# Another steady order for the first attention: scores and both mixes back to back, two turns fewer, GpSimd normalising the inputs

## The reference

```python
x = x + tanh(g_xattn[0]) * L0_xattn(ctx_1024, layernorm(x), mask, ...)   # the part that is changed
x = x + tanh(g_ffn[0])   * L0_ffn(layernorm(x), ...)                     # 16 experts, top 8 tokens each, and a shared one
x = x + tanh(g_xattn[1]) * L1_xattn(layernorm(x), ctx_1024, ctx_1024, ...)
x = x + tanh(g_ffn[1])   * L1_ffn(layernorm(x), ...)                     # ternary weights, 8 bit activations
```

```python
x = layer_norm(x, ...); latents = layer_norm(latents, ...)
q = latents @ Wq
k, v = split(concatenate([x, latents]) @ Wkv)
q = l2norm(q) * q_scale;  k = l2norm(k) * k_scale
sim = where(full_mask, einsum(q, k) * 8.0, -max)
out = einsum(softmax(sim), v)
return layer_norm(out @ Wo, ln_o_w, ln_o_b)
```

## Time and profile before

| | us |
|---|---|
| median of 3 runs | 406.26 (404.84 to 407.8) |
| span of the profiled execution | 402.5 |
| TensorE busy in it | 372.5 (93%) |
| VectorE busy | 328.7 (82%) |
| ScalarE busy | 257.7 (64%) |
| GpSimd busy | 226.0 (56%) |

### The profile page before, as it was taken

The page is one execution under the profiler, slowest core; times in us unless marked ns, Lnnn a source line. Parts: engine busy times, 40 slices in busy tenths (PEclk is TensorE's granted clock), DMA queues, the critical chain, the costliest instruction groups (busy, mean ns, idle before and its releaser), DMA issues. The chain is left out here.

```text
span 402.5 us, 10554 instructions
## 1 busy us (share of the span) xinstructions
PE 372.5 (93%) x3612; PEld 274.0 (68%) x3612; DVE 328.7 (82%) x925; ACT 257.7 (64%) x514; POOL 226.0 (56%) x372
## 2 busy tenths in 40 slices
PE   8799999999999999999999999999698999996766
PEld 8356666667666667668756888778477777775545
DVE  4889999899989999988483788564659999998995
ACT  2577777778777777776664222345377777777784
POOL 4564668766676666663322000056649999887850
PEclk9999999999999999999999999999999999999598
DMA  5969999700000000000000000000000000000003
GB/s 155 259 148 119 132 133 131 83 2 2 0 3 1 2 2 2 2 0 2 3 2 0 2 0 2 0 2 0 2 2 2 2 5 2 2 2 2 2 15 91
DMA packets 61283, 13.27 MB, mean 33 GB/s; under 512 B 51488, under 2 KB 60592, under 8 KB 61232
## 3 DMA queue, kind: packets, MB, share of 16 engines
q1 hardware_dynamic: 59776, 11.94, 19.6%
q10 hardware_dynamic: 1328, 0.66, 0.6%
q0 software_dynamic: 128, 0.00, 0.0%
HBM read 11.55 MB, written 1.05 MB: 31 GB/s over the span
## 5 line engine op out<-in xcount | busy, mean ns | idle before, releaser
L397 POOL TENSOR_TENSOR a_rn<-a_ssq,neghalf 128x8 f32<-128x8 f32 x48 | 79.0, 1653 | 29.8 <-DVE a_ssq L996 25.2
L996 DVE TENSOR_REDUCE a_ssq<-q_home 128x8 f32<-128x512 f32 x48 | 32.3, 672 | 6.5 <-ACT q_home L783 6.5
L91 POOL TENSOR_TENSOR moments<-moments,eps_row 128x1 f32<-128x1 f32 x32 | 6.2, 193 | 54.9 <-DVE moments L86 54.7
L486 PE MATMUL a_x<-wkv_a,a_kvT 128*128 128x512 f32 x64 | 34.5, 621 | 0.9 <-ACT kv_home L789 0.8
L789 ACT ACTIVATE kv_home<-a_x,maskcol 128x512 f32<-128x512 f32 x32 | 21.9, 684 | 19.1 <-PE a_x L486 19.1
L413 POOL TENSOR_TENSOR a_yr<-a_ymv,eps_row 128x1 f32<-128x1 f32 x16 | 3.0, 191 | 38.0 <-DVE a_ymv L1039 38.0
L1846 DVE TENSOR_REDUCE b_mx<-b_s 128x16 f32<-128x1024 f32 x16 | 19.6, 1223 | 5.3 <-PE b_s L1489 5.3
L1015 DVE TENSOR_REDUCE a_mx<-a_s 128x4 f32<-128x512 f32 x32 | 21.9, 686 | 2.0 <-PE a_s L512 1.9
L1343 POOL TENSOR_TENSOR b_k<-b_ksb,quad 128x256 f32<-128x256 f32 x32 | 18.9, 613 | 7.9 <-ACT b_ksb L1682 7.9
L531 PE MATMUL a_m<-kv_home,p_home 128*64 128x65 f32 x512 | 22.4, 228 | 0.7 <-issue 0.4
L801 ACT ACTIVATE kv_home<-a_m,cols 128x512 f32<-128x512 f32 x32 | 21.9, 685 | 0.8 <-PE a_m L500 0.7
(11 more groups left out here) (292 smaller groups left out, 1163.2 us busy)
## 6 DMA issues: line engine op xcount, KB each, us to landing
w_gu<-in_L_ffn_Wg_dram SPq DMA_DIRECT2D x4, 512.0 KB, 9.0
w_gu<-in_L_ffn_Wu_dram SPq DMA_DIRECT2D x4, 512.0 KB, 10.7
w_d<-in_L_ffn_Wd_dram SPq DMA_DIRECT2D x8, 256.0 KB, 7.8
out_dram<-xs SPq DMA_DIRECT2D x8, 128.0 KB, 1.8
xs<-in_x_dram SPq DMA_DIRECT2D x1, 640.0 KB, 11.3
cs<-in_ctx_dram SPq DMA_DIRECT2D x1, 640.0 KB, 11.1
wkv_a<-in_L_xattn_Wkv_dram SPq DMA_DIRECT2D x1, 512.0 KB, 7.7
nat<-in_L_ffn_w_dram SPq DMA_DIRECT2D x2, 256.0 KB, 3.1
```

The costliest lines, as they stand in the source:

```text
L397: nc.gpsimd.tensor_tensor(rn[:, tp, i, :], ssq[:, tp, i, :], neghalf[:, 0:H0], ALU.pow)\
L486: nc.tensor.matmul(p_x[:], kvT[:, tp, b * 2 * S:(b + 1) * 2 * S], wkv_a[:, INNER:2 * INNER], start=True, stop=True).then_inc(vproj_done, 1)
L996: nc.vector.tensor_reduce(ssq[:, tp, i, :], sq[:, i, :].rearrange("p (h d) -> p h d", h=H0), AX.X, ALU.add).then_inc(reduced, 1)
```

## The change

The loops of all four engines get another order, and `TURNS` ends two turns earlier (22 to 20). TensorE does both `probs_T` of tile s-2 and both `mix` of it in turn s, the mixes right behind the `scores` of tile s-1; `xT` of tile s+1 stands ahead of these scores. VectorE begins its turn with both `row_max`, both `attend`, both `shift`; the reductions and scales of tile s now lie in turn s itself, with `scale(s, 0)` right behind `reduce(s, 0)`. `normalise` moves from VectorE to GpSimd from the third tile on. For this the mean is kept with a minus sign and added. GpSimd does the powers of a tile in two turns, with `inverse_root` and `out_norm` between the first and the second. The diff, shortened:

```diff
-        TURNS = range(2, NT + 7)
+        TURNS = range(2, NT + 5)
...
+            def normalise(t, tp):
+                wait(pool, xT_done, t - 1 if t > 2 else t)
+                nc.gpsimd.tensor_scalar(xn[:, tp, 0, :], cs[:, t, :], moments[:, 0, t, 0:1], moments[:, 0, t, 1:2],
+                                        ALU.add, ALU.mult)
+                nc.gpsimd.tensor_scalar(xn[:, tp, 1, :], xs[:, t, :], moments[:, 1, t, 0:1], moments[:, 1, t, 1:2],
+                                        ALU.add, ALU.mult).then_inc(xn_ready, 1)
+
             inverse_roots(0)
             for i in range(3):
                 inverse_norm(0, 0, i)
             inverse_roots(1)
+            pool.wait_ge(norms_ready, 2)
+            normalise(2, 0)
+            inverse_norm(1, 1, 0)
+            inverse_norm(1, 1, 1)
             for s in TURNS:
+                if exists(s - 1, NT):
+                    inverse_norm(s - 1, (s - 1) % 2, 2)
+                if s == 5:
+                    inverse_roots(2)
+                    pool.wait_ge(norms_ready, 3)
+                if exists(s + 1, NT):
+                    normalise(s + 1, (s + 1) % 2)
+                if exists(s - 2, NT):
+                    weigh(s - 2, s % 2)
                 if exists(s - 4, NT):
                     add_bias(s - 4, s % 2)
...
+                if exists(s, NT):
+                    inverse_norm(s, s % 2, 0)
+                if exists(s - 5, NT):
+                    inverse_root(pool, s - 5).then_inc(root_ready, 1)
                 if exists(s - 4, NT):
                     out_norm(s - 4, s % 2)
+                if exists(s, NT):
+                    inverse_norm(s, s % 2, 1)
...
+                if exists(s - 2, NT):
+                    probs_T(s - 2, 1)
+                if exists(s + 1, NT):
+                    xT(s + 1, (s + 1) % 2)
                 if exists(s - 1, NT):
                     scores(s - 1, (s - 1) % 2)
+                if exists(s - 2, NT):
+                    mix(s - 2, s % 2, 0)
+                    mix(s - 2, s % 2, 1)
...
                 if exists(s - 2, NT):
                     exp(s - 2, 0)
+                    exp(s - 2, 1)
...
                 if exists(s - 2, NT):
                     row_max(s - 2, 0)
+                    row_max(s - 2, 1)
                 if exists(s - 3, NT):
                     attend(s - 3, 0)
                     attend(s - 3, 1)
+                if exists(s - 2, NT):
+                    shift(s - 2, 0)
+                    shift(s - 2, 1)
+                if exists(s - 1, NT):
+                    scale(s - 1, (s - 1) % 2, 2)
                 if exists(s, NT):
                     replace_masked(s, s % 2)
...
+                if exists(s, NT):
+                    reduce(s, s % 2, 0)
+                    scale(s, s % 2, 0)
+                    reduce(s, s % 2, 1)
+                if exists(s - 4, NT):
+                    write_output(s - 4, s % 2)
+                if exists(s - 5, NT):
+                    next_input(s - 5)
+                if exists(s, NT):
+                    reduce(s, s % 2, 2)
+                    scale(s, s % 2, 1)
```

More of the change, by code:

```diff
@@ L1117, in _ @@
             later = sum(GROUPS[2]) // 2
-            for s in TURNS:
-                if exists(s - 1, NT):
-                    reduce(s - 1, (s - 1) % 2, 0)
-                if exists(s, NT):
-                    for i, (first, _) in enumerate(GROUPS):
-                        if s == first:
-                            dve.wait_ge(norms_ready, i + 1)
-                    normalise(s, s % 2)
-                if exists(s - 1, NT):
-                    reduce(s - 1, (s - 1) % 2, 1)
-                if exists(s - 5, NT):
-                    write_output(s - 5, (s - 5) % 2)
-                if exists(s - 1, NT):
-                    scale(s - 1, (s - 1) % 2, 0)
+            reduce(1, 1, 0)
+            reduce(1, 1, 1)
+            scale(1, 1, 0)
+            reduce(1, 1, 2)
+            scale(1, 1, 1)
+            for s in TURNS:
                 if exists(s - 2, NT):
                     row_max(s - 2, 0)
-                if exists(s - 1, NT):
-                    reduce(s - 1, (s - 1) % 2, 2)
-                    scale(s - 1, (s - 1) % 2, 1)
-                if exists(s - 2, NT):
-                    shift(s - 2, 0)
+                    row_max(s - 2, 1)
                 if exists(s - 3, NT):
```

51 lines of the change are left out of this document (12 added, 39 removed).

## The result

| | before | after |
|---|---|---|
| median of 4 runs each, side by side, us | 405.55 (403.83 to 407.8) | 431.38 (429.09 to 433.23) |
| span of the profiled execution | 402.5 | 429.5 (that run: 432.3) |
| TensorE busy | 372.5 (93%) | 373.7 (87%) |
| VectorE busy | 328.7 (82%) | 322.9 (75%) |
| ScalarE busy | 257.7 (64%) | 255.5 (59%) |

After to before is 1.063 (95% interval 1.058 to 1.068): slower, near the 430 us of the prediction.

The account below looks back on a forecast made before the run. The prediction took TensorE to bound the kernel before, and a VectorE-GpSimd loop of 11.64 us after. Span 402.5 + 21.2 (through turn 15) + 2.4 (tail) = 426.1, plus 3.8 to the median: 430 us, range 419 to 438.

Parts of the forecast that it names:

- The loop: VectorE and GpSimd waits, key scale to key scale: 11.64 us a turn, 12.04 or 12.30 with weight transposes.
- A to R: VectorE, from key scale scale(s,1) to the next turn's query reduction reduce(s+1,0): 5.96 us without weight transposes.
- R to A: From query reduction over GpSimd's two powers and two pairs back to the key scale: 5.68 us.
- The sum along A: Key-scale starts added turn by turn through the first attention; turn 15's at 196.0 us, 21.2 later than before.
- A(2) to A(5): Key-scale starts of turns 2 to 5 on VectorE, forecast at 35.2, 45.8, 59.0 and 73.9 us.
- A(1): Start of turn 1's key scale on VectorE, after GpSimd's normalise and two powers: 25.9 us.
- the price of GpSimd's normalise: Two 128x128 operations on GpSimd: 1.20 us together, hidden in steady turns.
- the one-off work: Small work in turns 5 and 6 and turn 2's squares: 0 to 1.5 us together, taken as 0.7.
- Its own turn: TensorE's turn in the new order: from 10.79 us to 10.64, or 10.45 at best.
- The tail: Turn 15's key scale to last logits: near 27.3 us, 2.4 later than before, between -3 and +4.
- A(15): Start of turn 15's key scale on VectorE: 196.0 us, where before it was 174.78.
- The clock rival: TensorE idles more, its granted clock falls in the tail, matmuls double: 438 to 442 us; chance 8%.

Follow-up runs that it names:

- e1: Kernel after, with reduce(s,1) ahead of scale(s,0) on VectorE; 426.81 us, 1.051 of before.
- e2: Kernel after, with normalise put back on VectorE between reduce(s,0) and scale(s,0); 431.23 us, 1.064 of before.
- e3: Kernel after, with the powers of inverse_norm replaced by a multiplication (output differs); 405.2 us, 0.998 of before.
- y1: Kernel before, with turn_queries on TensorE moved behind both mixes instead of between them; 405.9 us, ratio 1.001.
- e4: Kernel before, with the powers of inverse_norm replaced by a multiplication (output differs); 405.28 us, ratio 0.997.
- e5: Kernel after, with GpSimd's inverse_root and out_norm behind the second power and VectorE's reductions, scales reordered; 433.37 us, 1.071 of before.
- x1: Kernel after, with both GpSimd powers first, VectorE reordered, write_output a turn later, one turn more; 428.19 us, 1.053 of before.
- x3: Kernel after reordered as in x1, plus read_output ahead of reduce(s,0), write_output and row_stats on VectorE; 415.52 us, 1.023 of before.
- y4: Kernel before with TensorE's whole new order, and on VectorE a reduction before row_max, read_output before a shift and next_input; 407.87 us, 1.004.

## Why the prediction was right, and where not

**The loop.** A to R was to be 5.96 us without weight transposes. Measured 129.59 - 123.21 = 6.38, of which 0.42 is a transpose (123.82 to 124.24): 5.96. R to A was to be 5.68 and is 5.59. So the turns are 11.97 and 12.23 where 12.04 and 12.30 were written down. That this loop sets them is shown by its pieces, which add up to the turn without a gap, and by e1 and e2 (moving or adding work in its gap changes a turn by 0.04 at most). That the powers make it so long is shown by e3. It worked because each piece had a row of its own in the trace of before; only their order was new.

**The sum along A**, from the timeline of VectorE: the key scales of turns 1, 7, 8 and, by the last row, 15:

```profile
25.21 0.69 DVE L1023 SCALAR_TENSOR_TENSOR q_home<-a_rn,a_y 128x512 f32<-128x512 f32 x1 [0.32 <-POOL a_rn L397]
...
98.23 0.69 DVE L1023 SCALAR_TENSOR_TENSOR q_home<-a_rn,a_y 128x512 f32<-128x512 f32 x1 [0.34 <-POOL a_rn L397]
110.98 0.69 DVE L1023 SCALAR_TENSOR_TENSOR q_home<-a_rn,a_y 128x512 f32<-128x512 f32 x1 [0.34 <-POOL a_rn L397]
...
195.80 0.69 DVE L1023 SCALAR_TENSOR_TENSOR q_home<-a_rn,a_y 128x512 f32<-128x512 f32 x1 [0.34 <-POOL a_rn L397]
```

The forecast had 25.9, 97.1, 110.0 and 196.0; in between, A(2) to A(5) were 35.04, 46.13, 59.28 and 74.19 against 35.2, 45.8, 59.0 and 73.9. That they lie so close is in part luck. A(1) came 0.7 earlier than forecast; turns 2 and 3 then took 9.83 and 11.09 where 9.25 and 10.55 were laid out. Of the 0.7 at A(1), 0.3 is that GpSimd was free earlier (normalise starts at 21.09, not 21.39). The step that failed is the price of GpSimd's normalise, taken as 0.60 for each of two from the earlier trace rows, which makes 0.3 more. It measured 0.44 from start to start:

```profile
124.79 0.45 POOL L419 TENSOR_SCALAR p_home<-cs,moments 128x128 f32<-128x128 f32 x1
125.22 0.45 POOL L421 TENSOR_SCALAR p_home<-xs,moments 128x128 f32<-128x128 f32 x1
```

The row that I took is an in-place multiplication by one column, not the same form. The Trainium skill, "GPSIMD Engine Reference", section 4.1 "Engine selection", calls one-input work there roughly line-rate. The measured 0.44 lies between the 0.34 that the prediction made of this and the 0.60 of the row. But 0.34 is VectorE's busy time; start to start the same operation took it 0.25, so GpSimd's took 1.8 times as long. In the steady turns neither price matters (e2). Of the one-off work that I lumped as 0.7, some shows in turns 6 and 7 (12.13 and 11.91 instead of 11.64): 0.76.

**TensorE.** Its own turn was bounded at 10.45 to 10.64; e3 shows 10.30, under both. The saving was mis-sized: 0.49, where the one row that was read gave 0.15 and the bound for all other changes of neighbours another 0.19. y1 shows that 0.19 of it comes from pulling the transposes out of the mixes. In the kernel after it never counted: of a turn of 11.97 TensorE lost 1.67, of which 1.0 ahead of `att_T` and 0.35 ahead of project(s,1).

**The tail.** The last next_input was to start 25.5 us after A(15), the last logits 27.3. From 195.80:

```profile
221.87 0.35 DVE L1062 TENSOR_SCALAR x_norm<-xs,moments 128x128 f32<-128x128 f32 x1 [0.35 <-POOL moments L93]
```

26.1, and the last logits start at 223.30, 27.5. The clock rival did not come true there: from 200 to 223.3 the granted clock is 1.00.

**Not foreseen: 3.4 us behind the logits.** "Everything behind the logits is unchanged and moves along" did not hold in the profiled run. From the last logits to the end it was 202.8 us before and 206.2 after. In the table of stretches of after, the stretch from 313.6 us, 90 us behind the last logits:

```profile
313.60:323.60 10.00, 9.71 (x90) 7.35 (x75) 4.42 (x7) 4.40 (x11) 2.68 (x5) 0.50 0.01 2
```

and before, as far behind:

```profile
290.00:300.00 10.00, 9.56 (x133) 8.04 (x118) 6.36 (x12) 6.21 (x17) 3.42 (x7) 0.83 0.01 2
```

0.50 is the lower of TensorE's two levels, 1.2 GHz, for the full 10 us, where before most of that stretch ran at 2.4. Just ahead, both kernels had TensorE busy 16.51 of 20 us.

The change doesn't force these 3.4 us. From the last logits to the end e1, which differs from the kernel after by the place of one reduction in the attention, took 202.9 us, and e2 203.4. The other way round, e3 and e4, whose medians agree within 0.1 us, took 200.7 us at a mean granted clock of 0.97 and 206.2 at 0.94. And one run of the kernel after, at a mean clock of 0.980 (the profiled run of before had 0.979), has a span of 426.6 us, where the forecast said 426.1. So it is mostly the clock of single executions. But the other three runs of the kernel after had 0.968 to 0.972, lower than most of before; whether it meets the lower level more often, and why the clock falls once more in one execution than in another, stays open.

The forecast of the median is therefore closer than its terms. The span was 3.4 us over, and against it I had allowed 3.8 us from span to median, where the median lay 1.9 over the span of the profiled run. That the two errors cancel in part is luck.

**What I had not seen at all** is the second loop. It was hidden 1 us behind the first, so it did not touch the forecast, but both first plans for mending the kernel (e5, x1) failed on it. x3 and y4 show it by cutting it.

## What to carry to other kernels

When a hand-written pipeline is put in another order, lay out the ring of waits that it closes, piece by piece from rows of the old trace, and compare its length with the busiest engine's turn; busy shares don't tell, since the chain of GpSimd, busy 55%, was half of what set the time here. The first long idle mark on the ring was not its cause: moving work into it changed nothing, only the length from release to release did. And before cutting one ring, measure the next longest one too; here it was 1 us shorter and ran through a PSUM bank that two stages share, and reading that bank earlier in the queue (x3) was worth more than the changes to the powers' order (e5, x1).
